# First chunk's attention scores with the keys down the partitions, and the second chunk's work in another order

## The reference

```
xn = layernorm(x)
# attention: its input is normalized again, times gamma, plus beta
h = layernorm(xn) * gamma + beta
q, k, v = h @ qkv[:, :512], h @ qkv[:, 512:1024], h @ qkv[:, 1024:]
attn = softmax(where(causal, q @ k.T / sqrt(512), -inf))
a = attn @ v @ o_proj + xn
# feed-forward
g = silu(xn @ w_gate) * (xn @ w_up)
f = keep_two_largest_of_four(g) @ w_down
out = xn + a + f
```

## Time and profile before

| | us |
|---|---|
| median of 3 runs (799.91 to 801.9) | 800.31 |
| profiled execution | 802.24 |
| its span, first to last instruction | 800.1 |
| PE busy | 786.4 |
| DVE, ACT, POOL busy | 610.4, 319.3, 16.7 |
| mean granted PE clock (share of full) | 0.993 |

### The profile page before, as it was taken

The page is one execution under the profiler, slowest core; times in us unless marked ns, Lnnn a source line. Parts: engine busy times, 40 slices in busy tenths (PEclk is TensorE's granted clock), DMA queues, the critical chain, the costliest instruction groups (busy, mean ns, idle before and its releaser), DMA issues.

```text
span 800.1 us, 9294 instructions
## 1 busy us (share of the span) xinstructions
PE 786.4 (98%) x3518; PEld 650.1 (81%) x3518; DVE 610.4 (76%) x964; ACT 319.3 (40%) x514; POOL 16.7 (2%) x26
## 2 busy tenths in 40 slices
PE   9999989699999999999999999999999999999998
PEld 6888878488888888888888888888888888888887
DVE  6978688576824688779989889799559558559786
ACT  5423251134312354563636436364334334335441
POOL 2010101001000000000000000000000000000000
PEclk9999999799999999999999999999999999999999
DMA  9541503630022335587426435497467262261002
GB/s 314 185 160 53 185 0 106 210 106 1 27 79 79 112 114 203 177 331 271 188 79 262 186 80 209 174 364 279 156 213 265 101 233 95 94 235 55 0 1 106
DMA packets 31611, 121.74 MB, mean 152 GB/s; under 512 B 3088, under 2 KB 3664, under 8 KB 29136
## 3 DMA queue, kind: packets, MB, share of 16 engines
q1 hardware_dynamic: 30272, 119.00, 40.7%
q10 hardware_dynamic: 1296, 2.16, 0.9%
HBM read 77.07 MB, written 44.07 MB: 151 GB/s over the span
## 4 chain that ended last, share of the span: by engine, by line
PE 95%; DMA 2%; issue 1%; DVE 1%; SPq 0%; ACT 0%; DVEq 0%
PE bank L962 13%; PE bank L960 13%; PE bank L961 13%; PE bank L699 9%; PE bank L701 9%; PE bank L700 9%; PE bank L1040 7%; PE bank L840 7%; PE bank L1042 7%; PE bank L1041 7%; DMA raw<-L_attn_qkv 1%; DMA spread<-row_stats 1%; DVE xh_raw L1540 0%; DVE v_lo L1574 0%; SPq L484 0%
## 5 line engine op out<-in xcount | busy, mean ns | idle before, releaser
L960 PE MATMUL bank<-X_hi,wset 128*128 128x512 f32 x448 | 174.4, 389 | 0.0
L962 PE MATMUL bank<-X_hi,wset 128*128 128x512 f32 x448 | 174.3, 389 | 0.0
L961 PE MATMUL bank<-X_lo,wset 128*128 128x512 f32 x448 | 174.3, 389 | 0.0
L962 PEld LDWEIGHTS bank<-X_hi,wset 128*128 128x128 f32 x448 | 84.1, 188 | 17.5
L961 PEld LDWEIGHTS bank<-X_lo,wset 128*128 128x128 f32 x448 | 84.1, 188 | 17.5
L960 PEld LDWEIGHTS bank<-X_hi,wset 128*128 128x128 f32 x448 | 84.1, 188 | 17.4 <-issue 0.2
L1040 PE MATMUL bank<-dw,hs_hi 128*128 128x512 f32 x224 | 87.2, 389 | 0.0
L1042 PE MATMUL bank<-dw,hs_lo 128*128 128x512 f32 x224 | 87.2, 389 | 0.0
L1041 PE MATMUL bank<-dw,hs_hi 128*128 128x512 f32 x224 | 87.1, 389 | 0.0
L1673 DVE TENSOR_TENSOR acc<-bank,acc 128x512 f32<-128x512 f32 x59 | 40.2, 688 | 40.1 <-PE bank L1042 39.6
L699 PE MATMUL bank<-zg,xT 128*128 128x512 f32 (+2 forms) x132 | 51.0, 387 | 0.0
(11 more groups left out here) (259 smaller groups left out, 1445.8 us busy)
## 6 DMA issues: line engine op xcount, KB each, us to landing
w_operands<-wset SPq DMA_DIRECT2D x8, 3584.0 KB, 13.9
wset<-w_operands SPq DMA_DIRECT2D x8, 3584.0 KB, 12.4
wsum<-w_units SPq DMA_DIRECT2D x28, 256.0 KB, 3.7
dw_raw<-L_ffn_w_down SPq DMA_DIRECT2D x14, 512.0 KB, 5.0
xw<-L_attn_x SPq DMA_DIRECT2D x4, 1024.0 KB, 9.8
xt_raw<-x_t SPq DMA_DIRECT2D x8, 512.0 KB, 7.5
xn_t<-xt_raw SPq DMA_DIRECT2D x8, 512.0 KB, 2.8
acc<-resid SPq DMA_DIRECT2D x2, 2048.0 KB, 9.3
```

The lines of the kernel that those rows point to most:

```text
L960: pe.matmul(dst[:], u[:, 0, :], x_hi, start=(first and kt == 0), stop=False, skip_group_check=True)
L961: pe.matmul(dst[:], u[:, 0, :], x_lo, start=False, stop=False, skip_group_check=True)
L962: last = pe.matmul(dst[:], u[:, 1, :], x_hi, start=False, stop=(kt == 1), skip_group_check=True)
```

## The change

It takes the query-tile way out: `WIDE` is now all four chunks, and `head`, `scores`, `exp`, `attend` and their helpers are gone (`exponentials`, `probs_hi`, `probs_lo`, `turn_probs`, `score_product` and others). Chunk 0 has four `wide` units (512, 384, 256 and 128 columns), three parts, and rules of its own: `largest` and `first_sums` run on one buffer instead of two halves. A unit's bank now follows the ring of products (`unit_bank`). Tile stores count in two semaphores, one for even tiles and one for odd ones, and all go through SP (before, the first four went through ACT's queue), so that two stores can be out before a load.

The list of steps is written anew between the first chunk's `v` and the third chunk's units. Chunk 1's `xh` and `z` now stand between chunk 0's second and third `meet`. Chunk 2's statistics move in front of chunk 0's `softmax`, and its `x_scale` and `row_turn` into it. `block_sum` moves from chunk 2's units to behind the last part of chunk 1's softmax, chunk 3's statistics from that softmax to behind the rows of tiles 4 and 5, and the third row turn stays behind unit 3, with `x_scale` of chunk 3 between the rows of tiles 6 and 7.

```
-    WIDE = (1, 2, 3)
-    OLD = TC * WIDE[0]
-    for i in range(OLD):
...
+    WIDE = range(NCH)
...
+    u = unit[0]
+    steps += [v[0][0], *u[0:2], x_scale[1], row_turn[1], row_copy[1], row_store[1], row_spread[1], *u[2:4], ("max_all", 0, 0), v[0][1],
+              *stat[2], x_stats[2], x_rstd[2]]
+    steps += softmax(0, {-1: [v[0][2]], 0: [v[0][3]]}, {1: [x_scale[2], row_turn[2], row_copy[2], row_store[2], row_spread[2]]})
+    steps += [xh_pre[1][0], *meet[0][0:2]]
+    steps += [step for k in range(KT) for step in (*xh_pre[1][k + 1:k + 2], xh[1][k], z_round[1][k])]
+    steps += [meet[0][2], *z[1], ("sum_turn", 0, 0), *rows_of[0][0], *rows_of[0][1], ("rows_load", 2, 0), ("rows_load", 3, 0)]
     u = unit[1]
...
+    steps += [*u[0:2], xn[1][0], xn[1][1], xn_store[1], xt_load[2], *rows_of[0][2], *rows_of[0][3], ("rows_load", 4, 0), ("rows_load", 5, 0),
+              *u[2:6], xh_pre[2][0], u[6], xh_pre[2][1], u[7], ("max_fold", 1, 0), ("max_all", 1, 0),
...
+    steps += softmax(1, {}, {2: [*z[2], *xn[0], xn_store[0]], 4: [("block_sum", 0, 0)]})
+    steps += [("sum_turn", 1, 0), *rows_of[1][0], *rows_of[1][1], ("rows_load", 6, 0), ("rows_load", 7, 0), *stat[3], x_stats[3], x_rstd[3], xt_load[3]]
     u = unit[2]
-    steps += [*u[0:2], ("block_sum", 0, 0), u[2], *rows_of[1][2], ("rows_load", OLD + 4, 0), u[3], *rows_of[1][3], ("rows_load", OLD + 5, 0),
+    steps += [*u[0:3], *rows_of[1][2], x_scale[3], *rows_of[1][3], ("rows_load", 8, 0), ("rows_load", 9, 0), u[3],
               row_turn[3], row_copy[3], row_store[3], row_spread[3], xn[2][0],
...
             def load_rows(n):
-                sp.wait_ge(resid_stored, 16 * (n - 1))
+                sp.wait_ge(resid_stored[n % 2], 16 * (n // 2))
...
+            def first_sums(j):
+
+                dve.wait_ge(exp_made, j + 1)
+                whole = sum_pair[0][:, 0, :]
+                if j == 0:
+                    sums_done[0] = step(nc.vector.tensor_copy(whole, raw_part(0, 0)))
+                    return
+                for u in wide_parts(0)[j]:
+                    some = whole[:, unit_cols(0, u):W]
...
```

279 lines of the change are left out of this document (79 added, 200 removed).

## The result

| | before | after |
|---|---|---|
| median, 11 runs each | 802.23 us | 804.10 us |
| profiled execution | 802.24 | 803.8 |
| its span | 800.1 | 801.8 |
| mean granted PE clock | 0.993 | 0.994 |

The ratio is 1.0032, with a 95% interval of 1.0018 to 1.0046: the changed kernel is slower by 0.3%, some 2.6 us at the ratio, 1.9 by the medians. That is just outside what the prediction called "the same", and 804.1 lies 0.1 above its range. The forecast had been 799.8.

A forecast was written before the change was run, and what follows sets the result against it. PE, busy 786.4 of 800.1 us, was taken as the bound. Terms +11.4, -1.6 and -10.3 gave -0.5, so 802.24 became 801.7, less 1.9 for the three-run median: 799.8, with an 8-in-10 range of 796.4 to 804.0.

The forecast's parts named there:

- Part 1, the first chunk: Up to chunk 1's scores: less PE work but three new waits and a fallen clock, +11.4 us.
- First wait: PE's first row turn waits for chunk 1's `x_scale`, queued on DVE behind the second unit's maximum: 2.0 us lost.
- Second and third: PE waits for chunk 2's `x_scale` at its row turn, then for DVE's copy before the products: 7.45 us together.
- the second change: POOL's change of code from chunk 0's maximum back to chunk 2's power, ahead of the second row turn: 8.3 us.
- Part 2, chunk 2's `z`: Wait for evacuating the last `v` tile shrinks from 2.5 to 0.85 us: -1.6.
- Part 3, the third row turn: Block sums moved earlier leave this turn just in time, 0.2 us allowed of the former 10.5: -10.3.
- The later chunks keep their order, and PE waits nowhere in them: Behind the third row turn: no new wait on PE, so no term in the sum.
- The prediction's own sign of being wrong: PE idle behind 145 us, or a second row turn starting before 64, would show the forecast wrong.
- The clock did not hold: Rival: PE's clock stays full after the long gap before the first products, saving 2.8 us: 797.0; chance 0.18.
- Dear code: Rival: each POOL code change costs 8.91 to 9.5 us, delaying the second row turn: 801.0 to 802.2; chance 0.14.
- The third row turn was not late: Rival: slow tile store and load make this turn late by 4.1 us: 803.7, or 806.5 with fallen clock; chance 0.11.
- things I haven't seen: Unnamed outcomes anywhere in the kernel, on either side of the forecast; chance 0.10.

The follow-up runs named there:

- experiments 8 and 11: Changed kernel with early `xn` stores and chunk 2's statistics and power before chunk 0's units, 796.32 us; 11 adds own-block copies and chunk 1's `x_scale` first, 794.31.
- experiment 8: Changed kernel with early `xn` stores, chunk 2's statistics and power ahead of chunk 0's units, its row turn behind the second `v` tile: 796.32 us.
- experiments 3 and 4: Changed kernel with SP's loads of tiles 8 and 9 behind chunk 3's row statistics, 803.41 us; 4 also has chunk 2's `xn` and stores two units earlier, 803.63.
- own_blocks_first: Changed kernel with earlier row statistics and `xn` stores, plus chunk 2's own blocks copied ahead of the waiting `xT` on ACT and DVE: 801.63 us.
- experiment 2: Changed kernel with only the block sums moved back between chunk 2's second and third units: 810.38 us, ratio 1.0116.
- old_first_chunk: Kernel before with only the part of the change behind the second chunk's units and tile stores counted in two semaphores: 797.41 us, ratio 0.9938.

## Why the prediction was wrong

**Part 1, the first chunk: right.** First wait 1.87 (2.0 taken). Second and third 6.74 and 0.57 of idle time with the turn between them, 7.8 by the start times (59.2 to 67.07), against 7.45. The turn at 66.12 against 66.0. Twelve slow matmuls and the turn, 0.2 each, lost 2.6, against 2.8. Chunk 1's scores at 87.65 against 87.6. POOL's idle time at the second change was 8.29 against 8.3, and this is luck in part: the 8.3 was taken from the DMA share of 0.55, but between 54.5 and 62.8 the share was 0.35, and in eight profiles of this order the idle time was 7.18 to 8.64. It mattered little, since POOL ended only 0.8 behind DVE (0.6 was expected). The Trainium skill (GPSIMD Engine Reference, section 2.1, Instruction dispatch) gives some 6 us for the first call into freshly loaded code. POOL's idle time on leaving for the maximum was 6.03 and 5.89 in experiments 8 and 11, near that figure, though the maximum's input came only 1.9 us before the start in experiment 8. On the way back it was longer, but took in time in which the statistics weren't ready, so no run decides whether the figure of the Trainium skill holds there.

**Part 2, chunk 2's `z`: right.** 0.76 idle and 1.0 by the start times, where 0.85 stood.

**Part 3, the third row turn: its own term right, the sentence behind it wrong.** The turn was on time (0.1 lost, 0.2 allowed), and 10.5 us came back. "The later chunks keep their order, and PE waits nowhere in them" is the step that failed. The order on PE is kept, but the waits are not: before, PE lost 10.5 us here while the transfers went on, and this loss was the cover for ACT's `xT` and the copies queued behind it. I had asked what becomes late behind the first wait and the second, not behind the one that goes. With it gone PE comes to the last copy with no slack left: 0.4 earlier than before, while `xT` and the copies are 1.8 later. I took the row statistics' place behind the loads on SP for the reason of the 1.8, but with them ahead of the loads `xT` began no earlier (experiments 3 and 4), so what makes the last `xn` store land later stays open. The sum had nothing for this wait; it costs 2.1. `own_blocks_first` takes it away by the copies' place and gives 2.0 back. The prediction's own sign of being wrong, an idle stretch behind 145 us, came true by this wait.

**The base.** The sum was -0.5 against the profiled 802.24, and I took another 1.9 off, because the three runs shown had a median of 800.31. Eleven runs of the same kernel have 802.23, and beside the later runs 802.18 to 802.79. The profiled execution was the typical one and the three runs were low. So of the 4.3 us between 799.8 and 804.1, 2.1 are the missed wait and 1.9 the base.

**The rivals.** The clock did not hold. Dear code did not come about: 8.29, under the 8.91 of the launch. The third row turn was not late; with the block sums in their old place it is (experiment 2), but by DVE's work on them and not by slow stores and loads, as the rival had it. The outcome, a wait that takes the place of the one removed, was in no rival: it was left to "things I haven't seen".

## What to carry to other kernels

When a change takes a long wait away, list what ran in its shadow on each other engine and when that ends, down to the next place where PE needs something of it. A short copy should not be queued behind an operation that waits for a transfer: two edits that issued the transfers 3 us earlier gained 0.7 at the most by the medians, and one that let four copies pass gained 2. And an edit that makes an engine earlier is to be judged only once the next wait downstream has been taken away. Last, one profile is one execution: that of `old_first_chunk` would have given the first chunk's cost as 10.1 us, where the medians say 6.7.
